# Graph attention over a 4096 x 4096 mask: half of each adjacency load issued by SP and half by ScalarE, from the thirteenth load on

## Chip, cores and metric

The kernel runs on one core of one Trainium2 chip. The metric is the device time of one execution in microseconds; the time before is 248.21 us, the median of three runs (247.85 to 251.82).

## The reference

One graph attention layer with a residual, N = 4096 nodes, F = 128 features. `adj` is int32, 64 MiB; nearly all the traffic from memory is this matrix.

```python
def ref(x, adj, W, a):
    h = maximum(layernorm(x), 0)
    Wh = h @ W
    e = (Wh @ a1)[:, None] + (Wh @ a2)[None, :]
    e = where(e > 0, e, 0.2 * e)
    e = where(adj > 0, e, -9e15)
    return x + elu(softmax(e, axis=1) @ Wh)
```

## The kernel before

**The work.** The 4096 output rows are cut into C = 4 chunks of 1024 rows, and for each chunk the 4096 columns of `adj` into U = 8 units of 512. For each unit the kernel loads the int32 mask (1024 rows x 512 columns, 128 partitions x 8 rows x 512 columns, 2 MiB), turns it into bytes on ScalarE (`to_bytes`, L529, an activation for each half of four rows), transposes it on TensorE (`turn`, L997), multiplies it on VectorE with the attention weights (`weights`, L796, four "words" a unit) and multiplies these on TensorE with the values (`product`, L1021 to L1023, 24 matmuls a word). The softmax weights are a maximum of two separable terms, so that a word is one VectorE instruction. Sums of a chunk are taken from the accumulators by VectorE (`take_sums`, L804), finished by GpSimd and ScalarE (`tail`) and stored.

**Sets.** In the last two chunks (`SETS` = 2, so chunks 2 and 3) the columns of units 4 to 7 are loaded otherwise: four sets h = 0 to 3 of 256 rows x 2048 columns, 2 MiB each, with the rows laid out so that a 32 x 32 block transposition on VectorE (`turn_set`, L776) can stand in for TensorE's. A set consists of four pieces of 32 partitions, 512 KB each: pieces 0 and 1 (partitions 0 to 63) are issued by SP (L322), pieces 2 and 3 (partitions 64 to 127) by ScalarE (L556). `set_to_bytes` (L547) converts a set in two activations. The first `turn_set` of a chunk waits until all four of its sets are converted. Chunk 2 takes its units in the order 0 to 7, chunk 3 in the order 0, 4, 5, 1, 6, 2, 7, 3.

**Order of loads.** All loads go through a ring of four slots `raw`. The list `LOADS` numbers them 0 to 31: 0 to 15 are the units of chunks 0 and 1, 16 to 19 units 0 to 3 of chunk 2, 20 is unit 0 of chunk 3, 21 to 24 are the sets of chunk 2, 25 to 28 the sets of chunk 3, 29 to 31 units 1 to 3 of chunk 3. Load n reuses the slot of load n - 4, so whoever issues it waits until ScalarE has converted that one (`act_bytes`). SP issues both halves of each unit as two DMAs of 1 MiB (`load_raw`, L316; half k holds rows 4k to 4k + 3 of all 128 partitions). After load 26 SP also issues the two loads of input rows of 512 KB (`load_rows`, L325). ScalarE issues its set pieces inside its own program (`load_sets`): behind the conversion of load 19 it waits for the first half of load 20 to land (L562) and issues its pieces of 21, 22 and 23; behind the conversions of 20 to 24 those of 24 to 28. SP, ScalarE and every other engine work through their instructions in order.

**Other work on ScalarE.** In the loop at L644, `tail(0)` stands behind load 13, `tail(1)` behind load 22, `store(0)` and `store(1)` behind 15 and 26. `square(g)` (L585), four activations that sum the squares of the high parts of the values for a range check, stand behind loads 14 to 17; SP waits for them before `load_rows`, since the rows overwrite part of `val`. The range check reads them at the end (L875).

Of the kernel before, what the change touches and what calls it, by code (L numbers as in the profile page):

```python
# [7 lines left out]
ACT = mybir.ActivationFunctionType  # L8
# [9 lines left out]
BT = 4  # L18
BLOCK = BT * P
CT = 2 * BT  # L20
# [16 lines left out]
RING = 4  # L37
QUARTER = 32
# [4 lines left out]
def bass_graph_attention(nc: bass.Bass, x: bass.AP, adj: bass.AP, w: bass.AP, a: bass.AP, out: bass.AP):  # L43
    N, F = x.shape
    T = N // P
    NB = N // BLOCK
    G = NB // 2
    C = N // CHUNK
    U = NB

    SETS = C - 2
    ORDER = [[*range(U)] if c <= SETS else [0, 4, 5, 1, 6, 2, 7, 3] for c in range(C)]

    LOADS = [(c, u, None) for c in range(SETS) for u in range(U)]
    LOADS += [(SETS, u, None) for u in range(4)] + [(SETS + 1, 0, None)] + [(c, None, h) for c in (SETS, SETS + 1) for h in range(4)]
    LOADS += [(SETS + 1, u, None) for u in range(1, 4)]
    RUNS = ((21, 29),)

    FILLED = [len([b for b in range(a % RING, a + 1, RING) if (LOADS[b][1] is None) == (LOADS[a][1] is None)]) for a in range(C * U)]
    V = F + 1  # L60
# [8 lines left out]
    adj_v = adj.rearrange("(c b p q) (u j) -> c b u p q j", b=2, p=P, q=BT, j=BLOCK)  # L69


    adj_lin = adj.rearrange("(c p t) (u j) -> c u p t j", p=P, t=CT, j=BLOCK)
# [3 lines left out]
    adj_set = adj.rearrange("(c h r t) (s k j) -> c s h k r t j", h=4, r=QUARTER, t=CT, k=4, j=BLOCK)  # L76
# [4 lines left out]
    with ExitStack() as ctx:  # L81
# [14 lines left out]
        val_set = moved.bitcast(F16).rearrange("p (t e v) -> p t e v", t=T // 2, e=2)  # L96
        val_set_u = moved.bitcast(U32).rearrange("p (t v) -> p t v", t=T // 2)
        word_set = moved.rearrange("p (t e v) -> p t e v", t=T // 2, e=2)
        raw = sb("raw", [P, RING, CT, BLOCK], I32)
# [3 lines left out]
        val = sb("val", [P, T, 2, VP], F16)  # L103
# [37 lines left out]
        squares = sb("squares", [P, G], F32)  # L141
        squared = first[:, 2 * CHUNK + T // 2 * VP:5 * CHUNK].bitcast(BF16).rearrange("p (t f) -> p t f", f=F)
# [45 lines left out]
        def group(g):  # L188
            return slice(g * CT, (g + 1) * CT)
# [107 lines left out]
        MOVES = 4 * 4  # L297
# [10 lines left out]
        @block.sync  # L308
        def _(sp):
            def load_x(b):  # L310
                sp.dma_start(x_sb[:, b * BT:(b + 1) * BT, :], x_v[b]).then_inc(x_in[b], 16)

            def load_raw(at, k):
                c, u, _ = LOADS[at]
                rows = adj_v[c, k, u] if c < SETS else adj_lin[c, u][:, k * BT:(k + 1) * BT]
                sp.dma_start(raw[:, at % RING, k * BT:(k + 1) * BT], rows).then_inc(raw_in[at % RING][k], 16)  # L316

            def load_set(at):

                c, _, h = LOADS[at]  # L320
                for k in SP_QUARTERS:
                    sp.dma_start(raw[k * QUARTER:(k + 1) * QUARTER, at % RING], adj_set[c, 1, h, k]).then_inc(set_in[at % RING], 16)  # L322

            def load_rows(c):
                sp.dma_start(rows_of(c).rearrange("p t f -> p (t f)"), x_lin[c]).then_inc(rows_in[c], 16)  # L325

            for b in range(4):
                load_x(b)
            load_raw(0, 0)
            for b in range(4, 6):  # L330
                load_x(b)
            load_raw(0, 1)
            for b in range(6, NB):
                load_x(b)
            for at in range(1, C * U):

                if LOADS[at][1] is None:
                    sp.wait_ge(act_bytes, 2 * (at - RING) + 1)
                    load_set(at)
                else:  # L340
                    for k in range(2):
                        if (at, k) == (RING, 0):
                            sp.wait_ge(first_bytes, 1)
                        elif at >= RING:
                            sp.wait_ge(act_bytes, 2 * (at - RING) + (1 if LOADS[at - RING][1] is None else k))
                        load_raw(at, k)
                if at == 26:

                    sp.wait_ge(words_free, SETS * U * BT)
                    sp.wait_ge(val_moved, MOVES)  # L350
                    sp.wait_ge(squares_ready, G)
                    load_rows(C - 2)
                    load_rows(C - 1)

            last = out_lin[C - 1].rearrange("p (t f) -> p t f", f=F)
            for k, (t0, t1) in enumerate(BANKS):
                sp.wait_ge(last_res, k + 1)
                sp.dma_start(last[:, t0:t1], rows_of(C - 1)[:, t0:t1]).then_inc(out_done, 16)

            sp.wait_ge(general_ready, 1)  # L360
            with sp.If(sp.value_load(general[0:1, 0:1], min_val=0, max_val=1) > 0):
                sp.wait_ge(out_done, 16 * OUT_DMAS)
                with sp.Fori(0, NB) as b:
                    with sp.Fori(0, BT) as q:
                        sp.wait_ge(gen_res, b * BT + q + 1)
                        sp.nop(nofuse=True)
                        sp.dma_start(adj_rows, adj_rows_v[bass.ds(b, 1), :, bass.ds(q, 1)].rearrange("g p q j -> (g p q) j")
                                     ).then_inc(gen_in, 16)
                        sp.dma_start(x_tile, x_v[bass.ds(b, 1), :, bass.ds(q, 1)].rearrange("g p q f -> (g p q) f")
                                     ).then_inc(gen_in, 16)  # L370
                        sp.wait_ge(gen_res, b * BT + q + 2)
                        sp.nop(nofuse=True)
                        sp.dma_start(out_rows_v[bass.ds(b, 1), :, bass.ds(q, 1)].rearrange("g p q f -> (g p q) f"), res_tile
                                     ).then_inc(gen_out, 16)
                        sp.wait_ge(gen_out, (b * BT + q + 1) * 16)
                        sp.nop(nofuse=True)

            sp.wait_ge(out_done, 16 * OUT_DMAS)
# [106 lines left out]
        def _(act):  # L485
# [62 lines left out]
                                         raw[:, at % RING, :, k * 256:(k + 1) * 256].rearrange("p t (m x) -> p m t x", m=2), ACT.Sign,  # L548
                                         scale=1.0, bias=step_bias[:, 0:1]).then_inc(act_bytes, 1)

            def load_set(at):

                c, _, h = LOADS[at]
                act.wait_ge(act_bytes, 2 * (at - RING) + 1)
                for k in ACT_QUARTERS:
                    act.dma_start(raw[k * QUARTER:(k + 1) * QUARTER, at % RING], adj_set[c, 1, h, k]).then_inc(set_in[at % RING], 16)  # L556

            def load_sets(at):

                for a0, a1 in RUNS:  # L560
                    if at == a0 - 2:
                        act.wait_ge(raw_in[(a0 - 1) % RING][0], FILLED[a0 - 1] * 16)  # L562
                        for a in range(a0, a0 + 3):
                            load_set(a)
                    elif a0 + 3 <= at + RING < a1:
                        load_set(at + RING)

            def row_copy(g, k):
                act.wait_ge(spread_ps, 2 * g + k + 1)
# [6 lines left out]
                                   aux.rearrange("p (q h l) -> p l q h", q=BT, l=2)).then_inc(grow_ready, 1)  # L576

            def square(g):
                if g == 0:
                    act.wait_ge(vh_ready, 2 + G - 1)  # L580

                    act.wait_ge(ht_ps, NB)
                else:
                    act.wait_ge(squares_ready, g)
                nc.scalar.activation(squared, val[:, group(g), 0, 0:F], ACT.Square, accum_out=squares[:, g:g + 1]  # L585
                                     ).then_inc(squares_ready, 1)

            centre(0)
# [41 lines left out]
            def tail(c):  # L630
                act.wait_ge(hp_ready, c + 2)
                nc.scalar.activation(neg[:], hp[:], ACT.Relu, scale=-1.0).then_inc(neg_ready, 1)  # L632
                act.wait_ge(neg_ready, c + 1)
                nc.scalar.activation(neg[:], neg[:], ACT.Exp, scale=-1.0).then_inc(ex_ready, 1)

            def store(c):
                act.wait_ge(res_ready, c + 1)
                if c < SETS:
                    act.dma_start(out_v[c].rearrange("p b q f -> p b (q f)"),
                                  rows_of(c).rearrange("p (b q) f -> p b (q f)", b=2)).then_inc(out_done, 16)  # L640
                else:
                    act.dma_start(out_lin[c], rows_of(c).rearrange("p t f -> p (t f)")).then_inc(out_done, 16)

            for at in range(U, C * U):  # L644
                c, u, h = LOADS[at]
                if u is None:
                    set_to_bytes(c, h)
                else:
                    for k in range(2):
                        to_bytes(c, u, k)  # L650
                load_sets(at)
                if at == 13:
                    tail(0)
                if 14 <= at < 14 + G:
                    square(at - 14)
                if at == 15:
                    store(0)
                if at == 22:
                    tail(1)
                if at == 26:  # L660
                    store(1)
            tail(2)
            store(2)

            nc.scalar.activation(warm[:], warm[:], ACT.Exp).then_inc(warm_ready, 1)
# [513 lines left out]
```

## Time and profile before

| | us |
|---|---|
| median of three runs | 248.21 |
| the profiled execution | 249.65 |
| its span, first to last instruction | 247.8 |
| TensorE (PE) busy | 222.3 |
| VectorE (DVE) busy | 199.0 |
| ScalarE (ACT) busy | 157.3 |
| GpSimd (POOL) busy | 81.1 |

Mean granted TensorE clock 0.965 of full speed. 70.32 MB were read from memory, 2.10 MB written.

The page of the profile gives busy time as a share of the whole span. The slices divide the span into 40 parts of 6.2 us and show for each the busy tenths of an engine, the granted clock and the rate of the DMA engines. In the timelines a row merges neighbouring instructions of one kind; the time in square brackets is the idle time of the engine before the first of them, with what ended it. "SPq" and "ACTq" rows are the issuing of DMAs by SP and ScalarE, which is not counted as busy time.

### The profile page before, as it was taken

The page shows a single profiled execution, that of the slowest core. Times are in us where ns is not written, and L with a number is a line of the kernel's source. Part 1 is how long each engine was busy: PE and PEld are TensorE (multiplying, and loading weights), DVE is VectorE, ACT ScalarE, POOL GpSimd, SP SyncE. Part 2 cuts the span into 40 slices and gives each one's busy share as a digit, 9 for nine tenths or more (in the row PEclk, how much of TensorE's full clock was granted, in tenths as well). Part 3 has the DMA queues.
Part 4 walks back from the last instruction along what each step waited for, and adds up shares of the span by engine and source line. Part 5 has one row for each costly group of instructions (what it writes and reads, how often), then busy time and mean ns, then how long its engine had stood idle before and what let it go on. Part 6 is the DMA issues. An engine that isn't in the chain of part 4 may idle for free.

```text
span 247.8 us, 8069 instructions
## 1 busy us (share of the span) xinstructions
PE 222.3 (90%) x3608; PEld 216.2 (87%) x3608; DVE 199.0 (80%) x266; ACT 157.3 (63%) x139; POOL 81.1 (33%) x68
## 2 busy tenths in 40 slices
PE   6969999699999999999999899508999999999990
PEld 2759998699999999999999899509999899999990
DVE  4999887546679988888789887029999999989866
ACT  3689836688899999978643367764574966300033
POOL 4647038895000209993000200930000300790000
PEclk9997999999999999999999999955999999999997
DMA  7999999999999999999999999999999980020002
GB/s 220 345 391 388 385 387 388 387 368 369 321 367 378 389 386 385 383 401 386 385 267 245 347 348 316 364 306 260 316 337 350 389 300 36 3 84 6 3 0 86
DMA packets 36791, 72.94 MB, mean 294 GB/s; under 512 B 1554, under 2 KB 2068, under 8 KB 36756
## 3 DMA queue, kind: packets, MB, share of 16 engines
q1 hardware_dynamic: 31568, 62.40, 72.8%
q10 hardware_dynamic: 5188, 10.03, 12.9%
q8 instruction: 28, 0.46, 0.8%
q14 instruction: 7, 0.06, 0.1%
HBM read 70.32 MB, written 2.10 MB: 292 GB/s over the span
## 4 chain that ended last, share of the span: by engine, by line
PE 38%; DMA 22%; ACT 15%; issue 11%; DVE 8%; POOL 4%; ACTq 2%; DVEq 0%; POOLq 0%
DMA raw<-in_adj_dram 20%; PE acc L1021 11%; PE acc L1023 10%; PE acc L1022 10%; ACT mask L529 8%; ACT second L547 3%; PE mask_t L997 3%; POOL second L415 2%; DVE words L796 2%; ACTq L556 2%; POOL val L418 2%; DVE stats L711 1%; DMA first<-in_x_dram 1%; PE acc L985 1%; ACT neg L675 1%
## 5 line engine op out<-in xcount | busy, mean ns | idle before, releaser
L796 DVE SCALAR_TENSOR_TENSOR words<-g_row,gq_word,mask_t 128x1024 f32<-128x1024 f32 x96 | 120.0, 1276 | 28.1 <-PE mask_t L997 13.3
L1021 PE MATMUL acc<-val,words 128*128 128x129 f16 x744 | 129.2, 221 | 10.4 <-DVE words L796 9.5
L1022 PE MATMUL acc<-val,words 128*128 128x129 f16 x744 | 129.2, 221 | 0.8 <-issue 0.8
L1023 PE MATMUL acc<-val,words 128*128 128x129 f16 x744 | 129.2, 221 | 0.0
L529 ACT ACTIVATE mask<-raw,step_bias 128x2048 uint8<-128x2048 int32 x47 | 92.0, 1997 | 17.4 <-issue 7.7
L1021 PEld LDWEIGHTS acc<-val,words 128*128 128x128 f16 x744 | 73.2, 98 | 10.8 <-DVE words L796 10.4
L1022 PEld LDWEIGHTS acc<-val,words 128*128 128x128 f16 x744 | 73.2, 98 | 1.1 <-issue 1.0
L1023 PEld LDWEIGHTS acc<-val,words 128*128 128x128 f16 x744 | 73.2, 98 | 0.0
L1021 PE MATMUL acc<-first,words 128*128 128x129 f16 x256 | 44.8, 222 | 0.0
L1022 PE MATMUL acc<-first,words 128*128 128x129 f16 x256 | 44.7, 222 | 0.0
L1023 PE MATMUL acc<-first,words 128*128 128x129 f16 x256 | 44.7, 222 | 0.0
L796 DVE SCALAR_TENSOR_TENSOR words<-g_row,first,mask_t 128x1024 f32<-128x1024 f32 x32 | 38.6, 1268 | 0.0
L444 POOL TENSOR_TENSOR hp<-num,rz 128x1024 f32<-128x1024 f32 x3 | 5.7, 1898 | 80.0 <-DVE rz L807 80.0
L547 ACT ACTIVATE second<-raw,step_bias 128x2048 uint8<-128x2048 int32 x12 | 23.5, 1992 | 9.9 <-DMA raw<-in_adj_dram 8.0
L997 PE MATMUL mask_t<-ident_b,mask 128*128 128x128 bf16 x384 | 26.1, 223 | 1.4 <-ACT mask L529 1.4
L1022 PEld LDWEIGHTS acc<-first,words 128*128 128x128 f16 x256 | 25.4, 99 | 0.0
L1021 PEld LDWEIGHTS acc<-first,words 128*128 128x128 f16 x256 | 25.4, 99 | 0.0
L1023 PEld LDWEIGHTS acc<-first,words 128*128 128x128 f16 x256 | 25.4, 99 | 0.0
L997 PEld LDWEIGHTS mask_t<-ident_b,mask 128*128 128x128 bf16 x384 | 23.2, 100 | 1.6 <-ACT mask L529 1.5
L448 POOL TENSOR_SCALAR hp<-hp 128x1024 f32<-128x1024 f32 x3 | 10.9, 3635 | 37.2 <-ACT neg L632 37.2
L776 DVE STREAM_TRANSPOSE mask_t<-second 128x1024 uint32<-128x1024 uint32 x6 | 7.5, 1253 | 11.1 <-ACT second L547 11.1
L547 ACT ACTIVATE mask<-raw,step_bias 128x2048 uint8<-128x2048 int32 x4 | 8.0, 2004 | 11.0 <-DMA raw<-in_adj_dram 11.0
(108 smaller groups left out, 205.3 us busy)
## 6 DMA issues: line engine op xcount, KB each, us to landing
raw<-in_adj_dram SPq DMA_DIRECT2D x48, 1024.0 KB, 14.3
raw<-in_adj_dram SPq DMA_DIRECT2D x16, 512.0 KB, 16.6
raw<-in_adj_dram ACTq DMA_DIRECT2D x16, 512.0 KB, 19.0
first<-in_x_dram SPq DMA_DIRECT2D x8, 256.0 KB, 5.9
out_dram<-first ACTq DMA_DIRECT2D x2, 512.0 KB, 11.6
val<-in_x_dram SPq DMA_DIRECT2D x2, 512.0 KB, 21.5
out_dram<-val ACTq DMA_DIRECT2D x1, 512.0 KB, 4.0
out_dram<-val SPq DMA_DIRECT2D x2, 192.0 KB, 1.9
```

Of the source, the lines that this page charges most:

```text
L415: nc.gpsimd.tensor_tensor(v32[:, g % 2], wh_sb[:, group(g), 0:F], dv[:, group(g)].unsqueeze(2).broadcast_to([P, CT, F]), ALU.mult).then_in ...
L418: nc.gpsimd.tensor_tensor(val[:, group(g), 1, 0:F], v32[:, g % 2], val[:, group(g), 0, 0:F], ALU.subtract).then_inc(vl_ready, 1)
L444: nc.gpsimd.tensor_tensor(hp[:], num[:, :, 0:F], rz[:].unsqueeze(2).broadcast_to([P, CT, F]), ALU.mult).then_inc(hp_ready, 1)
L448: nc.gpsimd.tensor_scalar(hp[:], hp[:], 0.0, -1.0, ALU.max, ALU.add).then_inc(pos_ready, 1)
L529: nc.scalar.activation(mask[:, mask_slot(c, u), k * BT:(k + 1) * BT], raw[:, at % RING, k * BT:(k + 1) * BT], ACT.Sign, scale=1.0, bias=st ...
L547: nc.scalar.activation(pair_bytes[PAIRS[c][k]][:, :, h], raw[:, at % RING, :, k * 256:(k + 1) * 256].rearrange("p t (m x) -> p m t x", m=2 ...
L776: nc.vector.transpose(maskt_quads[:, i % 2].rearrange("p (t h r) -> p t h r", h=4, r=QUARTER), pair_quads[PAIRS[c][m // 2]][:, m % 2]).the ...
L796: nc.vector.scalar_tensor_tensor(words[:, q], g_row[:, c * CHUNK:(c + 1) * CHUNK], word, bytes_t, ALU.max, ALU.mult).then_inc(words_ready, 1)
L997: last = nc.tensor.transpose(maskt_pairs[:, i % 2, h, t * P:(t + 1) * P], mask_pairs[:, mask_slot(c, u), t, :, h], ident_b[:])
L1021: nc.tensor.matmul(acc_tile(t), high, v[:, 0, 0:V], start=first and t % PT == 0, stop=False, skip_group_check=True)
L1022: nc.tensor.matmul(acc_tile(t), high, v[:, 1, 0:V], start=False, stop=False, skip_group_check=True)
L1023: last = nc.tensor.matmul(acc_tile(t), low, v[:, 0, 0:V], start=False, stop=False, skip_group_check=True)
```

## The change

From load 12 on SP issues only the first half of each unit (k = 0) and ScalarE the second, behind its own conversion of the load four places earlier; sets are shared as before. ScalarE no longer waits for load 20 to land before it issues set pieces; each is issued behind the conversion that frees its slot. In the list of loads the four sets of chunk 2 come ahead of unit 0 of chunk 3: they are loads 20 to 23, and the unit is load 24. The four squares move from behind loads 14 to 17 to behind `tail(2)`, ahead of `store(2)`; those of the last two groups read the copy `val_set`. SP's wait for them goes. `tail(1)` stands behind load 23 instead of 22.

```diff
     LOADS = [(c, u, None) for c in range(SETS) for u in range(U)]
-    LOADS += [(SETS, u, None) for u in range(4)] + [(SETS + 1, 0, None)] + [(c, None, h) for c in (SETS, SETS + 1) for h in range(4)]
-    LOADS += [(SETS + 1, u, None) for u in range(1, 4)]
-    RUNS = ((21, 29),)
+    LOADS += [(SETS, u, None) for u in range(4)] + [(SETS, None, h) for h in range(4)] + [(SETS + 1, 0, None)]
+    LOADS += [(SETS + 1, None, h) for h in range(4)] + [(SETS + 1, u, None) for u in range(1, 4)]
+    SHARED = U + RING
...
-                    for k in range(2):
+                    for k in range(2 if at < SHARED else 1):
...
-                    sp.wait_ge(squares_ready, G)
                     load_rows(C - 2)
                     load_rows(C - 1)
...
+            def load_half(at):
+
+                if SHARED <= at < C * U:
+                    c, u, h = LOADS[at]
+                    act.wait_ge(act_bytes, 2 * (at - RING) + 1)
+                    if u is None:
+                        for k in ACT_QUARTERS:
+                            act.dma_start(raw[k * QUARTER:(k + 1) * QUARTER, at % RING], adj_set[c, 1, h, k]).then_inc(set_in[at % RING], 16)
+                    else:
+                        rows = adj_v[c, 1, u] if c < SETS else adj_lin[c, u][:, BT:CT]
+                        act.dma_start(raw[:, at % RING, BT:CT], rows).then_inc(raw_in[at % RING][1], 16)
...
                 if g == 0:
                     act.wait_ge(vh_ready, 2 + G - 1)
-
-                    act.wait_ge(ht_ps, NB)
+                    act.wait_ge(val_moved, MOVES)
                 else:
                     act.wait_ge(squares_ready, g)
-                nc.scalar.activation(squared, val[:, group(g), 0, 0:F], ACT.Square, accum_out=squares[:, g:g + 1]
+                values = val[:, group(g), 0, 0:F] if g < 2 else val_set[:, group(g - 2), 0, 0:F]
+                nc.scalar.activation(squared, values, ACT.Square, accum_out=squares[:, g:g + 1]
                                      ).then_inc(squares_ready, 1)
...
-                load_sets(at)
+                load_half(at + RING)
                 if at == 13:
                     tail(0)
-                if 14 <= at < 14 + G:
-                    square(at - 14)
                 if at == 15:
                     store(0)
-                if at == 22:
+                if at == 23:
                     tail(1)
                 if at == 26:
                     store(1)
             tail(2)
+            for g in range(G):
+                square(g)
             store(2)
```

## Rows read from the trace of the kernel before

**Rows 1.** The page: busy tenths, granted clock and DMA in 40 slices

```profile
PE   6969999699999999999999899508999999999990
PEclk9997999999999999999999999955999999999997
DMA  7999999999999999999999999999999980020002
GB/s 220 345 391 388 385 387 388 387 368 369 321 367 378 389 386 385 383 401 386 385 267 245 347 348 316 364 306 260 316 337 350 389 300 36 3 84 6 3 0 86
```

**Rows 2.** The waits: engine, line, waited for: us in total, times, longest

```profile
DVE mask_t L776 <- ACT second L547: 11.1, 1, 11.1
...
PE acc L1021 <- DVE words L796: 9.5, 1, 9.5
```

**Rows 3.** The timeline of VectorE around the first set transposes: start, length

```profile
165.43 1.26 DVE L776 STREAM_TRANSPOSE mask_t<-second 128x1024 uint32<-128x1024 uint32 x1 [11.14 <-ACT second L547]
166.60 1.24 DVE L796 SCALAR_TENSOR_TENSOR words<-g_row,gq_word,mask_t 128x1024 f32<-128x1024 f32 x1
...
195.67 1.23 DVE L776 STREAM_TRANSPOSE mask_t<-mask 128x1024 uint32<-128x1024 uint32 x1
```

**Rows 4.** The timeline of TensorE around its two stops

```profile
158.20 0.22 PE L1023 MATMUL acc<-val,words 128*128 128x129 f16 x1
167.90 0.29 PE L1021 MATMUL acc<-val,words 128*128 128x129 f16 x1 [9.48 <-DVE words L796]
...
194.87 0.22 PE L1021 MATMUL acc<-val,words 128*128 128x129 f16 x1 [0.58 <-DVE num L804]
```

**Rows 5.** Busy time in stretches: length, engines (PE, PEld, DVE, ACT, POOL), clock, DMA share, GB/s

```profile
126.00:129.00 3.00, 3.00 (x57) 3.00 (x55) 2.84 (x3) 0.55 (x1) 0.00 (x0) 1.00 1.07 221
132.00:134.50 2.50, 2.50 (x48) 2.50 (x45) 2.42 (x3) 0.29 (x1) 0.00 (x0) 1.00 1.08 205
134.50:162.00 27.50, 23.09 (x405) 22.74 (x402) 16.50 (x16) 17.80 (x11) 8.67 (x4) 1.00 1.06 345
162.00:192.00 30.00, 24.10 (x387) 24.11 (x388) 26.51 (x23) 17.08 (x9) 1.53 (x1) 0.83 1.05 312
162.30:167.90 5.60, 0.00 (x1) 0.01 (x1) 2.47 (x3) 3.10 (x2) 1.24 (x1) 0.50 1.05 285
167.90:172.50 4.60, 4.60 (x43) 4.60 (x44) 4.60 (x5) 2.00 (x1) 0.00 (x0) 0.50 1.06 263
194.87:241.34 46.47, 46.47 (x818) 46.26 (x818) 42.76 (x46) 14.91 (x15) 13.05 (x5) 1.00 0.23 85
```

**Rows 6.** The timeline of ScalarE: conversions and issues from load 19 to load 28

```profile
122.65 3.90 ACT L529 ACTIVATE mask<-raw,step_bias 128x2048 uint8<-128x2048 int32 x2 [2.26 <-PE mask_t L997]
126.93 7.17 ACTq L556 DMA_DIRECT2D raw<-in_adj_dram  x6
...
142.18 3.90 ACT L547 ACTIVATE second<-raw,step_bias 128x2048 uint8<-128x2048 int32 x2 [4.07 <-DMA raw<-in_adj_dram]
...
190.12 2.00 ACT L547 ACTIVATE mask<-raw,step_bias 128x2048 uint8<-128x2048 int32 x1 [3.27 <-DMA raw<-in_adj_dram]
192.03 1.99 ACT L547 ACTIVATE second<-raw,step_bias 128x2048 uint8<-128x2048 int32 x1
```

**Rows 7.** Issues of loads: KB and us to landing; then one issue, ns min/median/max

```profile
raw<-in_adj_dram SPq DMA_DIRECT2D x48, 1024.0 KB, 14.3
...
L316 SPq DMA_DIRECT2D raw<-in_adj_dram x48: 368/2268/5902, 2.6 to 191.0; - x48
...
L556 ACTq DMA_DIRECT2D raw<-in_adj_dram x16: 571/626/3827, 126.9 to 166.0; - x16
```

**Rows 8.** Timelines of ScalarE and TensorE: a square, a store, the late idle, a turn

```profile
97.80 1.04 ACT L585 ACTIVATE first<-val 128x1024 bf16<-128x1024 f16 x1
98.75 0.19 ACT L585 ACTIVATION_READ_ACCUMULATOR first<-val 128x1 f32 x1
...
101.70 0.43 ACTq L639 DMA_DIRECT2D out_dram<-first  x1
...
147.84 1.06 PE L997 MATMUL mask_t<-ident_b,mask 128*128 128x128 bf16 x16
...
220.80 0.20 ACT L665 ACTIVATE warm<-warm 128x1 f32<-128x1 f32 x1 [7.97 <-POOL val L455]
```

More of the change, by code:

```diff
@@ L549, in set_to_bytes @@
                                          scale=1.0, bias=step_bias[:, 0:1]).then_inc(act_bytes, 1)
[L551 to L566, printed above, removed]
+            def load_half(at):
[8 more added lines that the diff above has]
+                        act.dma_start(raw[:, at % RING, BT:CT], rows).then_inc(raw_in[at % RING][1], 16)
             def row_copy(g, k):
```

## The prediction

> **What bounds the kernel now.** The slices of the page come first: TensorE is at nine tenths or more nearly everywhere, with a hole at 155 to 168 us where its clock falls too, and the DMA engines stay busy from the start to 200 us while their rate sags from 385 to 250-350 GB/s after 124 us [rows 1]. The waits name the hole: VectorE waits 11.1 us once for a ScalarE conversion (L547), and TensorE waits 9.5 us once for VectorE [rows 2]. The timelines place it. VectorE's first set transpose of chunk 2 starts at 165.43, since it needs all four sets of that chunk converted [rows 3]; TensorE stops at 158.42 and restarts at 167.90 [rows 4]. From 167.9 to 172.5 it runs at half clock [rows 5], 2.3 us of lost work. After that TensorE is full to 241.3 but for 0.58 us [rows 4, 5]. So the hole costs 9.5 + 2.3 = 11.8 us of the end, and it is a wait for data: ScalarE waits for set loads at 142.18 and again later [rows 6].
>
> Why the sets are late: from 126 to 134.5 us the DMA moves 205 to 221 GB/s, from 134.5 to 162 it moves 345 [rows 5]. In the first stretch SP's half of the sets runs alone, because ScalarE only issues its half at 126.93, after the wait for load 20 at L562 [rows 6]. A set piece goes to 32 partitions, and SP's two go to partitions 0 to 63 alone. Lost: 8.5 us x (345 - 210) / 345 = 3.3 us of transfer.
>
> **The change, part by part.** A load is 2.10 MB (two of 1024 KB) [rows 7].
>
> *Order.* The sets of chunk 2 become loads 20 to 23, unit (3,0) becomes 24; the sets of chunk 3 stay 25 to 28. Half of load 20 landed at 126.9 [rows 6], so the row loads before it end near 126.9 - 2.7 = 124.2. They come at the DMA's own rate (385 GB/s [rows 1]), which the split can't raise. Both engines can issue set 20 as soon as unit 16 is converted, well before that, so no stretch is left at 210. Four sets at 345 GB/s take 8.39 / 0.345 = 24.3 us: the last lands at 148.5, and with 3.9 us of conversion [rows 6] it is ready at 152.4. TensorE runs dry at 158.4; transpose and next word take 2.4 us (165.43 to 167.8 [rows 3]), so anything before 156.0 leaves no hole. The first stall goes, with 3.6 us in hand.
>
> *What is late next.* The first transpose of chunk 3 also waits for four sets, 25 to 28, and they are loads as before. Now it starts at 195.67 [rows 3], the last set having landed at 190.12 and been converted by 194.02 [rows 6]: only 1.65 us spare. With 11.8 us taken off, TensorE would need the word behind that transpose at 194.87 + 72 matmuls x 0.0568 - 11.8 = 187.1 (0.0568 us is 46.47 us over 818 matmuls [rows 5]), so the last conversion would have to end by 184.7. Landing of load 28, estimated twice. By bytes: after 148.5 come 5 loads, the input rows of 1.05 MB and a store of 0.52 MB, 12.06 MB; 13.5 us at 345 GB/s move 4.66, the other 7.40 at 312 (the rate from 162 to 192 [rows 5]) take 23.7: 185.7. By difference: 190.1 less the 3.3 us recovered is 186.8. I take the later, since a row load now stands in the middle of the sets. No row has that mixture: at the 263 GB/s of 167.9 to 172.5, when the input rows ran between sets [rows 5], its 2.1 MB cost 1.9 us more than at 345; at 385 they gain 0.6. The 1.1 us between my two estimates lie in the middle. Plus 3.9 us of conversion: 190.7. TensorE gets its word at 193.1, 6.0 us after it ran dry. In the old hole the clock was down 3.9 us after TensorE stopped (158.42 to 162.3 [rows 4, 5]), so 6.0 us should bring it down again and cost the same 2.3 us. VectorE is busy 42.8 of the 46.5 us after 194.87 [rows 5], so TensorE stays the bound behind it. Sum: 11.8 - 6.0 - 2.3 = 3.5 us gained.
>
> *Row halves on ScalarE.* ScalarE now issues the second half of 12 row loads (12 to 19, 24, 29 to 31); SP loses these. SP's issue of such a half lasts 0.37 to 5.90 us, median 2.27, because it blocks behind a full queue; ScalarE's set issues 0.57 to 3.83 [rows 7]. ScalarE's store at 101.70 took 0.43 to issue [rows 8]. For loads 12 to 19 I take the lower end for the path: even 8 x 2.3 = 18 us would be hidden, since unit 19 is converted at 126.6 and TensorE turns it at 147.84 [rows 6, 8], and the loads themselves wait a median 14.3 us in their queue. Half a load no longer lands 2.7 us ahead of the other, so each conversion ends up to 2 us later; same cover. For loads 27 to 31 the cover is thin: see the slower rival. At the median, 2.3 us for load 31 after conversion 27 (about 184.6) ends at 186.9, just as load 28 lands, so I count nothing.
>
> *Squares.* Four of 1.04 + 0.19 us leave the row phase, where ScalarE had slack, and come after tail(2). There ScalarE idles 7.97 us, to 220.80, for GpSimd [rows 8], and 4.9 us fit in. VectorE reads them only behind its last word, 16 us later, so even without that cover they cost nothing. SP's removed wait on them ended when the fourth square did, long before the load of input rows. *tail(1)* goes behind one more conversion: 2.1 us ahead of conversion 24, whose user, TensorE's turn of (3,0), comes some 15 us later. Store(1) waits for GpSimd either way.
>
> **The Trainium skill against the trace.** DMA: Bandwidth & Descriptors, Rules for kernel authors, says that splitting a transfer over partition halves, or over SP and ACT, gains nothing, since all run on the same 16 engines. For 128-partition halves the trace agrees (385 GB/s from one queue [rows 1]); for 32-partition pieces it differs, 210 against 345 [rows 5]. SBUF — State Buffer, Door 1, gives a reason: partitions 0 to 63 share eight of 16 ports. By the first rule nothing is recovered, and the sum is the rival below.
>
> **Rivals.**
> 1. *The wait only moves.* No transfer time is recovered, load 28 lands at 190.1 as now. The word comes at 194.0 + 2.4 = 196.4, 9.3 us late: 11.8 - 9.3 - 2.3 = 0.2 us, 248.0. For it: the DMA engines never rest, total bytes are the same. Against: the two stretches of [rows 5]. The rule above would give this. Chance 0.2.
> 2. *No second hole.* Load 28 lands by 180.8. That is 20.5 MB in 56.6 us, 361 GB/s, more than any long stretch with sets shows (345). Gain 11.8: 236.4. In between, a hole under 3.9 us keeps the clock: 238 to 241. Chance 0.18.
> 3. *Slower: ScalarE blocks on its own issues.* Its queue is in order, and between conversions 23 and 28 it now has five loads to issue (27, 28, then row halves 29, 30, 31), where before SP issued the rows. At the upper ends (4.45 us a set pair, 5.90 a row half) the chain from 152.4 is 4.5 + tail 2.1 + 3.9 + 4.5 + 3.9 + 5.9 + 3.9 + 5.9 + 3.9 + 5.9 + 3.9 = 200.7 for conversion 28. The word comes at 203.1, 16.0 us late: 11.8 - 16.0 - 2.3 = -6.5, 254.7. It decides from conversion 28 at 194.2 (no gain) and makes 2% at 199.2. Against: the median issue is far shorter. Chance 0.12.
>
> The forecast itself has 0.5.
>
> **The numbers.** The profiled execution took 249.65 with a span of 247.8; the median of the runs is 248.21. The sum is a difference, so I take it off the median: 248.2 - 3.5 = 244.7. If the clock stays up in the second hole it is 242.4. The forecast's own range, with load 28 landing at 184.5 to 189.5, is 240 to 247.5. The range 238.5 to 250 takes in the first rival, most of the second and the mild part of the third. A change of 2% (5 us) is about what a measurement tells from none: faster takes the second rival and four tenths of the forecast, 0.38; slower the upper half of the third and a little for transfers disturbed by the row load among the sets, 0.1; within 2% the rest, 0.52.
>
> **What would show it.** Right: VectorE's wait before its first transpose of chunk 2 near zero; no stretch at 210 GB/s around 130 us; a new wait of about 6 us before the first transpose of chunk 3, at about 190, released by a conversion (L547) that waited for a load; TensorE dry once, near 187, at half clock after it. Wrong: a wait still standing at 155 (set transfers far under 345); no wait at 184 to 190 (transfers over 355); ScalarE idle with issues of 3 to 6 us between conversions 25 and 28, the load having long landed.

## The result: 1% slower, with the first wait shortened and a second one in its place

The changed kernel takes 252.31 us, the median of 20 runs (249.84 to 255.72); the kernel before, run beside it, 250.38 (247.64 to 253.06, 20 runs). The ratio is 1.0095 with a 95% interval of 1.0062 to 1.0127: slower, by less than 2%. The forecast was 3.5 us faster. Medians in this document are of all runs, while ratios compare only the runs within 1.5% of the fastest of their kernel.

The page of the changed kernel, to be held against [rows 1]:

```profile
span 250.0 us, 8068 instructions
...
PE   5969999699999999999999999699985199999990
...
PEclk9997999999999999999999999999999579999998
DMA  6999999999999999999999999999999981020002
GB/s 208 347 392 388 384 387 384 388 365 374 302 356 381 387 385 386 387 387 382 330 372 369 343 281 265 306 295 266 303 311 294 392 342 49 3 82 7 3 0 85
```

The hole at 155 to 168 us has shrunk to one slice at six tenths, and another has opened at about 190 to 200, with the clock down in it and behind it. The weak stretch of the DMA at 124 to 136 has gone (372, 369). A short dip stands ahead of its place, at 119 to 125 (330, where before moved 386), and a longer weak stretch runs from 144 to 194: 281, 265, 306, 295, 266, 303, 311, 294.

The timelines of VectorE and TensorE, which answer to [rows 3] and [rows 4]; L771 is the set transposition (L776 before), L1016 the first matmul of a product:

```profile
157.72 1.26 DVE L771 STREAM_TRANSPOSE mask_t<-second 128x1024 uint32<-128x1024 uint32 x1 [4.14 <-ACT second L546]
...
196.72 1.26 DVE L771 STREAM_TRANSPOSE mask_t<-mask 128x1024 uint32<-128x1024 uint32 x1 [9.06 <-ACT second L546]
```

```profile
160.19 0.23 PE L1016 MATMUL acc<-val,words 128*128 128x129 f16 x1 [2.48 <-DVE words L791]
...
199.18 0.29 PE L1016 MATMUL acc<-val,words 128*128 128x129 f16 x1 [8.18 <-DVE words L791]
```

VectorE's first wait falls from 11.14 to 4.14 us, TensorE's stop from 9.48 to 2.48 and its clock no longer falls there: 9.3 us won. In front of the first transposition of chunk 3, where VectorE waited for nothing before, it now waits 9.06 us, TensorE stops 8.18 us, and its clock is down for 4.1 us after it. The PE rows show the first matmul after each stop. Busy time in stretches (columns as in [rows 5]):

```profile
117.00:123.00 6.00, 6.00 (x110) 6.00 (x108) 4.66 (x4) 4.38 (x4) 1.74 (x3) 1.00 1.06 328
123.00:141.00 18.00, 18.00 (x322) 18.00 (x320) 15.52 (x17) 11.31 (x6) 1.90 (x1) 1.00 1.05 371
141.00:159.00 18.00, 16.70 (x296) 16.53 (x293) 11.51 (x10) 9.96 (x6) 0.00 (x0) 1.00 1.06 279
165.00:177.00 12.00, 11.45 (x200) 11.10 (x198) 12.00 (x11) 4.11 (x3) 3.87 (x2) 1.00 1.05 270
183.00:192.00 9.00, 6.97 (x121) 6.65 (x118) 4.62 (x7) 3.95 (x3) 1.90 (x1) 1.00 1.06 279
199.18:203.30 4.12, 4.12 (x39) 4.12 (x40) 4.12 (x4) 2.88 (x3) 0.00 (x0) 0.50 1.05 408
```

Sets alone, shared by two queues, move at 371 GB/s. Then come three stretches at 270 to 279, and the DMA share is 1.05 or 1.06 all through: the engines are not short of work, their packets take longer. What is in flight tells them apart: from 141 unit (3,0), the row load that now stands between the sets (load 24: ScalarE's half was issued at 137.5 and landed 23.6 us later, at 161.1); from 165 the input rows (issued at 151.0, landed about 25 us later); from 183 the row halves of load 29 and a store. The timeline of ScalarE, the answer to [rows 6], gives the landings (a conversion that waited for a DMA starts when it lands):

```profile
153.79 3.90 ACT L546 ACTIVATE second<-raw,step_bias 128x2048 uint8<-128x2048 int32 x2 [4.13 <-DMA raw<-in_adj_dram]
157.72 1.50 ACTq L557 DMA_DIRECT2D raw<-in_adj_dram  x2
159.27 1.06 ACT L627 ACTIVATE neg<-hp 128x1024 f32<-128x1024 f32 x1 [1.58 <-issue]
...
183.59 3.76 ACTq L634 DMA_DIRECT2D out_dram<-first  x1
187.78 2.00 ACT L546 ACTIVATE mask<-raw,step_bias 128x2048 uint8<-128x2048 int32 x1 [4.72 <-issue]
...
191.70 0.47 ACTq L560 DMA_DIRECT2D raw<-in_adj_dram  x1
192.79 2.00 ACT L546 ACTIVATE mask<-raw,step_bias 128x2048 uint8<-128x2048 int32 x1 [1.12 <-DMA raw<-in_adj_dram]
```

The last set of chunk 2 landed at 153.79 (148.5 forecast), the last of chunk 3 at 192.79 (186.8). Issues by ScalarE, for [rows 7]: set pieces, then row halves.

```profile
L557 ACTq DMA_DIRECT2D raw<-in_adj_dram x16: 571/772/3982, 113.7 to 165.8; - x16
...
L560 ACTq DMA_DIRECT2D raw<-in_adj_dram x12: 374/464/642, 73.4 to 191.7; - x12
```

### The profile page after: what moved, and what is told of

Its sections match the earlier page's. It is cut to its first block, busy times and chain, and to the rows that moved or that the text cites. A ratio compares the mean times of both kernels' runs of the same rounds, so it can differ in the third digit from the quotient of the medians.

```text
span 250.0 us, 8068 instructions
## 1 busy us (share of the span) xinstructions
PE 222.6 (89%) x3608; PEld 216.0 (86%) x3608; DVE 199.0 (80%) x266; ACT 158.1 (63%) x139; POOL 81.0 (32%) x68
## 4 chain that ended last, share of the span: by engine, by line
PE 26%; DMA 24%; ACT 20%; issue 14%; ACTq 6%; POOL 4%; DVE 4%; SPq 1%; DVEq 0%; POOLq 0%
DMA raw<-in_adj_dram 24%; ACT mask L528 15%; PE acc L1016 7%; PE acc L1017 7%; PE acc L1018 7%; ACTq L557 3%; PE mask_t L992 3%; POOL second L414 2%; DVE words L791 2%; POOL val L417 2%; ACT second L546 2%; ACTq L560 2%; SPq L311 1%; PE acc L980 1%; ACT neg L670 1%
## 5 line engine op out<-in xcount | busy, mean ns | idle before, releaser
L1016 PE MATMUL acc<-val,words 128*128 128x129 f16 x744 | 129.2, 221 | 12.0 <-DVE words L791 10.7
L1016 PEld LDWEIGHTS acc<-val,words 128*128 128x128 f16 x744 | 73.2, 98 | 12.7 <-DVE words L791 12.2
L1016 PE MATMUL acc<-first,words 128*128 128x129 f16 x256 | 44.7, 222 | 0.8 <-DVE words L791 0.8
L447 POOL TENSOR_SCALAR hp<-hp 128x1024 f32<-128x1024 f32 x3 | 10.9, 3634 | 57.1 <-ACT neg L627 57.1
L1016 PEld LDWEIGHTS acc<-first,words 128*128 128x128 f16 x256 | 25.3, 99 | 1.4 <-DVE words L791 1.4
L667 ACT ACTIVATE second<-num,rz 128x128 f32<-128x128 f32 x6 | 2.0, 389 | 18.6 <-DVE rz L885 18.6
```

The source lines that it names most:

```text
L447: nc.gpsimd.tensor_scalar(hp[:], hp[:], 0.0, -1.0, ALU.max, ALU.add).then_inc(pos_ready, 1)
L1016: nc.tensor.matmul(acc_tile(t), high, v[:, 0, 0:V], start=first and t % PT == 0, stop=False, skip_group_check=True)
```

## Experiments

Two theories. **Mixture**: a load to all 128 partitions and set pieces to 32 partitions of one half disturb each other while both are in flight, and the change puts such a load in the midst of the sets. **Rivals**: dealing row loads over two queues is itself slow; or only the order of arrival counts. "Before" ran beside each group, at a median of 249.7 to 250.8 us. Most groups have four runs of a kernel. Stretches, waits and landings are those of the one profiled execution of each.

**e1: the order undone.** The change, with unit (3,0) as load 20 again.

```diff
-    LOADS += [(SETS, u, None) for u in range(4)] + [(SETS, None, h) for h in range(4)] + [(SETS + 1, 0, None)]
-    LOADS += [(SETS + 1, None, h) for h in range(4)] + [(SETS + 1, u, None) for u in range(1, 4)]
+    LOADS += [(SETS, u, None) for u in range(4)] + [(SETS + 1, 0, None)] + [(SETS, None, h) for h in range(4)]
+    LOADS += [(SETS + 1, None, h) for h in range(4)] + [(SETS + 1, u, None) for u in range(1, 4)]
...
-                if at == 23:
+                if at == 24:
                     tail(1)
```

> Undoes the order alone: unit (3,0) is load 20 again and the sets are 21 to 28 in one run; halves stay shared, squares at the end, tail(1) behind the last set of chunk 2. Mixing theory (a 128-partition row load between 32-partition set pieces holds the DMA at about 280 GB/s for some 18 us): no slow stretch at 141 to 159, sets at about 370 GB/s, load 28 lands near 186 instead of 192.8, the second wait shrinks from 9.1 to about 3 us or less, and the time falls 4 to 7 us below the changed kernel, below before too. Rival (sharing row halves over two queues is what slows): time stays within 1 us of the changed kernel, with a slow stretch left. Rival (only the order of arrival counts, the rate is what it is): the first wait grows by 5 us and the second stays, time 1 to 3 us above the changed kernel.

Measured: 245.35 us (244.68 to 245.74), ratio to before 0.982 (0.9753 to 0.9886). Its stretches:

```profile
123.00:141.00 18.00, 18.00 (x322) 18.00 (x320) 15.52 (x17) 10.77 (x6) 1.90 (x1) 1.00 1.06 331
141.00:159.00 18.00, 16.47 (x292) 16.29 (x288) 10.00 (x8) 11.89 (x8) 0.00 (x0) 1.00 1.05 371
```

The slow stretch at 141 is gone; a short one is left where unit (3,0) meets the first sets. Load 28 lands at 187.5 and VectorE does not wait at the second place. The first wait is 7.6 us. Halves were still shared, so sharing is not what slows; the order alone cost the change 7 us.

**e2: sharing of the row loads undone.** The change, with both halves of every unit on SP.

```diff
-                    for k in range(2 if at < SHARED else 1):
+                    for k in range(2):
...
-                if SHARED <= at < C * U:
+                if SHARED <= at < C * U and LOADS[at][1] is None:
```

> Undoes the sharing of row loads alone: SP issues both halves of every unit, ScalarE only its set pieces; new order, squares at the end. Mixing theory: load 24 still stands among the sets, so the rate from 141 to 159 stays near 280 GB/s or falls lower, since SP's queue then has twice as much row data between its set pieces as ScalarE's has none; time within 2 us of the changed kernel or above it. Sharing theory: the slow stretch goes and the time falls 4 us or more. ScalarE's own issue time (0.4 to 0.6 us a row half) is worth nothing by both.

Measured: 265.69 us (264.29 to 267.92), ratio 1.0645 (1.0551 to 1.0738). The stretches from 114 on:

```profile
114.00:123.00 9.00, 9.00 (x163) 9.00 (x161) 7.21 (x6) 3.67 (x2) 0.04 (x1) 1.00 1.06 273
123.00:141.00 18.00, 16.48 (x293) 16.30 (x289) 14.38 (x15) 6.01 (x3) 1.90 (x1) 1.00 1.06 270
141.00:159.00 18.00, 17.82 (x315) 17.64 (x312) 11.27 (x9) 10.83 (x6) 0.00 (x0) 1.00 1.07 261
```

The sharing rival falls: sharing the row halves is worth 13 us in this order. The reason I see is that it keeps the two queues in step. Here ScalarE's queue has only sets in it and runs ahead, so that sets and rows mix from 114 on; the three rates fit this, and no run tests it by itself.

**e3: row loads dealt by partitions.** Loads 16 to 31 that are units: SP writes partitions 0 to 63, ScalarE 64 to 127, each all eight rows. A conversion waits for both, and SP, like ScalarE, issues its part once the load four places earlier is converted whole.

```diff
-                sp.dma_start(raw[:, at % RING, k * BT:(k + 1) * BT], rows).then_inc(raw_in[at % RING][k], 16)
+                if c >= SETS:
+                    sp.dma_start(raw[0:64, at % RING], adj_lin[c, u][0:64]).then_inc(raw_in[at % RING][0], 16)
...
-                        act.dma_start(raw[:, at % RING, BT:CT], rows).then_inc(raw_in[at % RING][1], 16)
+                            act.dma_start(raw[64:128, at % RING], adj_lin[c, u][64:128]).then_inc(raw_in[at % RING][1], 16)
```

> Row loads from 16 on are cut by partitions instead of rows: SP loads partitions 0 to 63, ScalarE 64 to 127, as the set pieces are; same bytes, same order as the changed kernel, 1 MiB each. Mixing theory: each queue then writes only its own half of the partitions, whatever shape is in flight, so load 24 costs what a set costs; rate from 141 to 159 near 370 GB/s, load 23 lands near 148, load 28 near 188, both waits shrink by about 4 us, time 4 to 5 us below the changed kernel. The price: row loads 16 to 19 at 370 instead of 387 GB/s, 1 us in all. If the mixture of shapes is not the cause: within 1 us of the changed kernel.

Measured: 246.77 us (243.35 to 248.64), ratio 0.9774 (0.9669 to 0.9879).

```profile
GB/s 213 348 391 387 386 386 387 387 384 384 339 350 383 391 386 372 295 368 370 371 396 358 351 355 369 363 318 279 309 355 362 368 345 87 3 3 90 3 0 88
...
141.00:159.00 18.00, 16.55 (x293) 16.38 (x290) 12.55 (x11) 11.57 (x8) 0.63 (x1) 1.00 1.05 364
165.00:177.00 12.00, 11.45 (x200) 11.10 (x197) 12.00 (x12) 7.55 (x4) 1.91 (x1) 1.00 1.05 305
...
151.75 3.90 ACT L551 ACTIVATE second<-raw,step_bias 128x2048 uint8<-128x2048 int32 x2 [2.44 <-DMA raw<-in_adj_dram]
...
185.80 2.00 ACT L551 ACTIVATE mask<-raw,step_bias 128x2048 uint8<-128x2048 int32 x1 [0.71 <-ACT second L551]
```

Same bytes, same order, same two queues, same size of DMA: 364 GB/s instead of 279. Load 23 lands 2.0 us earlier than in the change (151.75), load 28 at least 7.0 us (by 185.80). What counts is how the loads in flight are cut. The cut also changes which rows of the matrix are read at one time, and no run separates the reading side from the partitions written. The second wait falls from 9.06 to 4.11 us and TensorE's stop from 8.18 to 3.23, with its clock up until the tail. The four runs lie apart (243.35, 244.94, 248.59, 248.64) and the profiled one is the fastest, so the 8 us to the change that the ratios give (0.9774 against 1.0095) are its best case; the medians are 5.5 us apart.

This kernel has a mixture of its own, and no set is in it. Load 16 is the first to be cut by partitions and follows loads cut by rows: in the slice from 97 to 103 us the rate falls to 295 GB/s, where the change moved 386 and 387. In e6, e12 and e4 the same slice has 277, 279 and 254.

**e4: the input rows by partitions too.** The edits of e3, with:

```diff
-                sp.dma_start(rows_of(c).rearrange("p t f -> p (t f)"), x_lin[c]).then_inc(rows_in[c], 16)
+                sp.dma_start(rows_of(c).rearrange("p t f -> p (t f)")[0:64], x_lin[c][0:64]).then_inc(rows_in[c], 16)
...
+                if at == 22:
+                    act.wait_ge(words_free, SETS * U * BT)
+                    act.wait_ge(val_moved, MOVES)
+                    for cc in (C - 2, C - 1):
+                        act.dma_start(rows_of(cc).rearrange("p t f -> p (t f)")[64:128], x_lin[cc][64:128]).then_inc(rows_in[cc], 16)
```

> As the kernel before in this list (row loads cut by partitions), and the two loads of input rows too: SP partitions 0 to 63, ScalarE 64 to 127, 256 KB each, issued by ScalarE behind its pieces of load 26. Mixing theory: the stretch of 265 to 280 GB/s from 165 to 177 goes as well, 12 us at 270 become 8.7 us at 370, load 28 lands near 185; time 2 to 3 us below e3. If the slow stretch is due to the 4 KB packets or to the memory side: as e3.

Measured: 243.66 us (242.76 to 247.7), ratio 0.9742 (0.9664 to 0.9821). No gain over e3 can be told: the ratios differ by 0.3% and their intervals overlap, and the median is 3.1 us lower only because two of e3's four runs took 248.6. The stretch came up only to 326:

```profile
165.00:177.00 12.00, 12.00 (x202) 12.00 (x200) 12.00 (x11) 9.64 (x6) 5.79 (x3) 0.94 1.05 326
...
151.56 3.22 ACTq L658 DMA_DIRECT2D val<-in_x_dram  x2
```

The second row is ScalarE's issue of the two small loads: 3.22 us ahead of the conversion that the first wait hangs on, and that wait is 5.91 us here against 3.10 in e3. TensorE stops for 4.25 us and then runs at half clock from 161.3 to 165.5.

**e5: input rows and store(1) out of the way.** The change, with them behind load 31 and conversion 30.

```diff
-                if at == 26:
+                if at == C * U - 1:
...
-                if at == 26:
+                if at == 30:
                     store(1)
```

> The changed kernel with the two loads of input rows issued behind load 31 instead of 26 and store(1) behind conversion 30 instead of 26; row loads cut by rows as in the change. Mixing theory: the stretch at 165 to 177 (270 GB/s) and 1.6 MB leave the way of loads 27 and 28, the row load 24 among the sets stays. Load 28 lands at about 184 instead of 192.8, the first wait stays near 4 us, the second falls to about 1 us: 244 to 246 us against 252 of the changed kernel. If input rows and store were only bytes and disturbed nothing: 4.3 us earlier, 247 to 248.

Measured: 245.03 us (244.24 to 246.59), ratio 0.9865 (0.9776 to 0.9954). Load 28 lands at 187.9, and VectorE waits 5.28 us first and 3.72 us second, against 4 and 1 expected. 165 to 177 now runs at 342 GB/s, 141 to 159 still at 284. The time fell inside the expected 244 to 246 although load 28 landed 3.9 us later than expected, so the hit is in part luck. The granted clock of this execution, in the 40 slices of its page:

```profile
PEclk9999999999999999999999999979999989999998
```

TensorE stopped for 3.63 us and for 2.84 us, and behind each it ran at about half clock for a while (0.52 from 160.6 to 164, 0.50 from 195 to 198). So a stop shorter than the 3.23 us of e3 can be followed by the low clock.

**e6 and e12: both cures.** The edits of e3 and e5 together.

> Both cures together: row loads from 16 on cut by partitions (SP 0 to 63, ScalarE 64 to 127), input rows behind load 31, store(1) behind conversion 30; new order of loads. Mixing theory: 360 to 370 GB/s without a gap from 123 to 195, load 23 lands by 150, load 28 by 177; no second wait, first wait at most 1 us, PE stops only for tenths; time 238 to 240 at a kernel before of 249.7. If what slowed was the memory side or the queue's order and not the destinations: not better than e3 (246.8 median, span 241.5).

> The same kernel as e6, for a narrower interval: row loads from 16 on by partitions, input rows behind load 31, store(1) behind conversion 30. By the mixture theory 239 to 241 again, ratio 0.955 to 0.965 to before.

Measured: 239.85 us (239.3 to 242.7), ratio 0.9704 (0.9521 to 0.9888), and again 239.65 (239.4 to 241.32), ratio 0.9632 (0.9557 to 0.9708). Of e6:

```profile
123.00:141.00 18.00, 18.00 (x322) 18.00 (x320) 15.90 (x16) 12.30 (x7) 1.90 (x1) 1.00 1.05 381
141.00:159.00 18.00, 16.97 (x301) 16.80 (x299) 12.97 (x11) 11.98 (x8) 0.72 (x1) 1.00 1.05 371
...
155.60 1.26 DVE L778 STREAM_TRANSPOSE mask_t<-second 128x1024 uint32<-128x1024 uint32 x1 [2.69 <-ACT second L551]
...
185.46 1.22 DVE L778 STREAM_TRANSPOSE mask_t<-mask 128x1024 uint32<-128x1024 uint32 x1
```

No second wait, and TensorE keeps its full clock from 6.6 us to the tail. Load 23 lands at 151.7 and load 28 at 181.3, 1.7 and 4.3 us later than expected. This version beats both kernels.

**e7: the set pieces dealt otherwise.**

```diff
-        SP_QUARTERS, ACT_QUARTERS = (0, 1), (2, 3)
+        SP_QUARTERS, ACT_QUARTERS = (0, 2), (1, 3)
```

> The changed kernel with the set pieces dealt otherwise: SP takes pieces 0 and 2, ScalarE 1 and 3, so that in step both queues write the lower half of the partitions and then both the upper half. If a 32- or 64-partition destination limits the rate (port theory), the pure set stretch of 123 to 141 falls from 371 to near 210 to 280 GB/s and the time rises to 265 or more. If two queues are what makes 371 (and one queue's limit is what made 210), nothing changes: 371 GB/s, 252 us.

Measured in a single execution: 265.73 us.

```profile
123.00:141.00 18.00, 18.00 (x322) 18.00 (x320) 15.51 (x17) 9.05 (x5) 1.90 (x1) 1.00 1.07 275
141.00:159.00 18.00, 16.82 (x292) 16.35 (x289) 10.02 (x8) 8.25 (x5) 0.00 (x0) 1.00 1.06 267
```

Two queues as in the change, and 275 instead of 371 GB/s. So 371 needs the pieces dealt so that the two queues, taken in step, write different halves of the partitions.

**e8: squares and tail(1) alone**, on the kernel before.

```diff
-                if 14 <= at < 14 + G:
-                    square(at - 14)
...
-                if at == 22:
+                if at == 23:
                     tail(1)
...
             tail(2)
+            for g in range(G):
+                square(g)
             store(2)
```

> The kernel before with the squares behind tail(2), reading val_set for the last two groups, without SP's wait for them, and tail(1) behind load 23; loads and who issues them as before. Both theories: nothing, within 0.5% of before (squares idle under GpSimd's 8 us wait; tail(1) 2.1 us behind the conversion of load 23, ahead of 24, the last set that the first wait needs: at most 2 us longer there).

Measured: 251.97 us (248.45 to 255.94, ten runs), ratio 1.0045 (0.9975 to 1.0115): no difference that can be told.

**e9: sets issued early, the rest as before.** The edits of e1 and e2 together, so that against before only ScalarE's wait for load 20 (and the squares) is missing. ScalarE's first set pieces are issued at 114.5 instead of 126.9.

> Old order of loads and all row halves on SP, as before; but ScalarE issues its set pieces behind the conversion that frees the slot, without the wait for load 20 to land (L562); squares at the end. Mixing theory: ScalarE's queue, with only sets in it, runs ahead of SP's, which still has rows 18 to 20, so that sets and rows are mixed from about 115 on: under 280 GB/s there, later SP's set pieces alone near 210, the first wait at least as long as before (11 us), the second above 5 us; 255 to 265. If the wait at L562 was just lost time (my prediction's view): the 3.3 us come back, 245 to 247.

Measured: 258.4 us (254.83 to 260.93), ratio 1.0347 (1.0254 to 1.044). The profiled execution is the shortest of the four.

```profile
114.00:123.00 9.00, 9.00 (x163) 9.00 (x161) 7.25 (x6) 4.33 (x3) 0.00 (x0) 1.00 1.06 331
123.00:141.00 18.00, 18.00 (x322) 17.98 (x320) 15.77 (x16) 6.01 (x3) 1.90 (x1) 1.00 1.06 271
```

The wait that I had booked as 3.3 us lost was what kept sets and rows apart. The first wait is 10.9 us, the second only 0.7 where I had expected over 5; TensorE stopped twice more, for 1.26 us until 144.3 and for 2.29 us until 154.0, while conversions of row units waited for their loads.

**e10: the best kernel with the old order.** The edits of e1, e3 and e5.

> The best kernel so far (row loads by partitions, input rows and store(1) late) with the old order, unit (3,0) as load 20. Mixing theory: the order then only says what is late: the same rate near 370, the last set of chunk 2 lands one load (5.7 us) later, near 157 instead of 151.7, so the first wait is about 8 us against 2.7 and TensorE loses 6 us and some clock; no second wait; 244 to 246 against 239.9. That is what the new order is worth once the mixture is gone.

Measured: 247.34 us (245.67 to 248.5), ratio 0.9853 (0.9763 to 0.9943). The first wait is 11.0 us, 3 more than expected (346 GB/s from 141 to 159, not 370). With the mixture gone the new order is worth 247.3 - 239.9 = 7.5 us; with it, by e1, it costs 7. That the same edit changes sign is the plainest sign that the order by itself is not what slows (the input rows are late in the first pair and not in the second, too).

**e11: before with input rows and store(1) late.** The edit of e5 on the kernel before.

> The kernel before with only the input rows behind load 31 and store(1) behind conversion 30. Before had no second wait (1.65 us spare), so bytes taken out of the way of loads 27 and 28 buy nothing; the input rows come after the first stop. Both theories: within 1% of before.

Measured: 251.23 us (247.52 to 252.92) beside 250.76 of before: no difference that four runs can tell, as a kernel without a second wait should show.

## Why the prediction was wrong

- **Reading of the hole, and that the first stall goes: right in kind.** Booked 11.8 us, got 9.3. The last set landed 5.3 us late against 3.6 in hand, and TensorE ran dry at 157.7 instead of 158.4, so 2.48 us of the stop remained.
- **A second wait in front of chunk 3, released by a conversion, TensorE at half clock behind it: right**, at the place forecast, though TensorE ran dry at 191.0 and not 187.1. Booked 6.0 + 2.3; measured 8.2, 0.4 more at take_sums and 4.1 us at half clock (2.1): 10.7, with three stops of 0.28 us besides. 9.3 - 10.7 - 0.8 = -2.2 us, which is the shift of TensorE's last matmul (241.3 to 243.6). The forecast gave 0.52 to a time within 2% of before, and so it came, but only because 9.3 us won and 11.5 lost nearly cancel.
- **The step that failed: the price of "a row load now stands in the middle of the sets".** I bounded it at 1.9 us, 2.1 MB at 263 GB/s, and took 1.1. It slowed everything in flight: from 141 to 159 the rate was 279 instead of 371, 18 x 92 / 371 = 4.5 us, and it stayed low around the input rows (270, against 305 in e3). With all loads of the matrix from 16 on cut alike, e3 lands load 28 by 185.8, the change at 192.8: 7.0 us instead of 1.1. The low rate around the input rows stood in [rows 5], and I charged it to the new load by its own bytes, not to its neighbours in the queues. e1, e3 and e6 show this term.
- **A second term was off: the start of the sets.** Of the 5.3 us at load 23, 3.3 were there at set 20 already: it landed at 133.6, against 124.2 + 6.1 = 130.3 by the forecast, and load 24 was issued only at 137.5. So 124.2 was too early an end for the row loads. A part is the dip at 119 to 125, where the first set pieces meet the last row loads; the rest I did not trace. The three sets behind set 20 took 20.2 us, against 18.2 by the forecast and 18.6 in e3: that part is the mixture.
- **From load 23 to load 28 the forecast of 38.3 us held (39.0) by luck.** It was made of 345 and 312 GB/s, rates of before with mixtures of their own in them. In e3 the same five loads take 34 us.
- **"3.3 us recovered" was half the story.** The stretch at 210 went, but e9 shows that ending it by issuing early, alone, costs 3.5%. It works only with the row halves shared (e2).
- **The rule weighed against the trace.** The Trainium skill, DMA: Bandwidth & Descriptors, Rules for kernel authors, says that halves of the partitions gain nothing. That does not hold for this mixture: e3 differs from the change by that cut alone and is 5.5 us faster by the medians. What agrees is the Trainium skill, SBUF — State Buffer, Door 1, on the ports of partitions 0 to 63: e7, 275 against 371 GB/s.
- **The rivals.** The first, that the wait only moves, came nearest in kind, but for another reason and on the wrong side of zero. The third, ScalarE blocked by its issues, did not decide: its row halves took 0.46 us in the median and 0.64 at most. Its store at 183.59 blocked 3.76 us and held conversion 27 back, but load 28 landed after that (192.79). The second rival let a hole under 3.9 us keep the clock: e3's did (3.23 us), e5's did not (3.63 and 2.84).
- **Squares at nothing: right** (e8 within noise). **Row halves at nothing: right for the path** (conversions of the row phase in time for TensorE), but sharing them is what the new order needs (e2).

The range 238.5 to 250 missed 252.3: the sums behind it priced the mixture by the bytes of one load, and transfers disturbed by it had a little of a chance and no sum.

## What to carry to other kernels

When DMA engines are saturated, ask of each load not only how many bytes it has but which partitions each queue is writing beside it: here it paid to keep the two queues on different halves and in step, and to cut the one differently shaped load the same way or to move it out of the stretch. Moving the data that one wait needs to the front takes it from the next; compute the next wait's slack (here 1.65 us) before counting a gain. Loads needed late, like the input rows here, belong behind the last urgent one.

## What the runs showed of the hardware

- 2 MiB loads from memory: 381 to 390 GB/s by rows over all 128 partitions, from one queue or two; 371 by pieces when the two queues, in step, write opposite halves; 275 when they are dealt pieces of the same half; 261 to 284 when a 128-partition load is in flight with set pieces; 254 to 295 when loads cut by rows meet loads cut by partition halves (e3, e4, e6, e12, at about 100 us). The DMA share reads 1.05 to 1.08 in all these stretches, so it doesn't show the loss; the rate does.
- 205 to 221 GB/s in the kernel before from 126 to 134.5 us. ScalarE's pieces were issued there from 126.9 on, but the first of them landed at 139.2, the first of SP's at 132.1; that SP's pieces, for partitions 0 to 63, moved alone is read from these landings.
- TensorE's clock went to half at or after stops of 8.2 and 9.5 us, of 4.25 (e4), 3.63 and 2.84 (e5), and 2.08 (the change, at 18 us: 0.62 from 18.1 to 22), and stayed up through stops of 3.23 (e3) and 2.48 (the change, at 160). The length of the stop alone does not tell which.
- Not settled: why one mixed load slows its neighbours for 18 us rather than for its own 5 to 6. It was itself in flight for most of that time, until 161.1. The views give rates for all queues together, not for single DMA engines, and no run separated them.
